# A six-layer fused kernel: causal attention's first sources made inside masked attention, experts' scores reordered by one tile, context loads issued earlier

## The reference, cut to what matters

```python
x = x + cross_attention(norm(x), ctx)          # 16 heads, 257 keys
x = x + state_space(norm(x))
x = x + soft_experts(norm(x))                  # 16 experts x 16 slots
x = x + masked_attention(norm(x), ctx, mask)   # one head, 257 keys
x = x + causal_attention(norm(x))              # 16 heads over 32 rows
x = x + routed_linear(norm(x))                 # one of 8 matrices for a row
```

## Time and profile before

| | us |
|---|---|
| times of the runs shown | 984.61, 985.24, 1930.26 |
| median | 985.24 |
| time of the profiled execution | 986.62 |
| its span | 984.8 |
| TensorE busy | 815.8 (83%) |
| VectorE busy | 726.6 (74%) |
| ScalarE busy | 563.4 (57%) |
| GpSimd busy | 201.6 (20%) |

### The profile page before, as it was taken

One profiled execution on the slowest core, in us unless ns is written; L12 is line 12 of the kernel. 1 busy time (PEld: TensorE's weight loads), 2 busy tenths in 40 slices (PEclk: granted clock), 3 DMA queues, 4 the chain that ended last, 5 costly groups with the idle time before them and its releaser, 6 DMA issues. The chain is left out here.

```text
span 984.8 us, 25493 instructions
## 1 busy us (share of the span) xinstructions
PE 815.8 (83%) x9286; PEld 448.7 (46%) x9286; DVE 726.6 (74%) x2428; ACT 563.4 (57%) x1419; POOL 201.6 (20%) x216
## 2 busy tenths in 40 slices
PE   5899999998867687887764577789698799999887
PEld 2577777776323233333231255456466334343343
DVE  5688888886389999989999588256565376767856
ACT  3798889889666658458415167445243533333345
POOL 1376676666000000000000012000310000000036
PEclk9999999999978789789867799799699899999989
DMA  8111111100000000000000250400183000000001
GB/s 251 34 40 46 37 43 37 38 21 2 1 0 0 1 0 1 1 1 1 0 1 1 82 99 1 173 4 4 44 322 150 1 1 1 1 1 1 1 13 32
DMA packets 23422, 36.67 MB, mean 37 GB/s; under 512 B 5668, under 2 KB 19748, under 8 KB 21156
## 3 DMA queue, kind: packets, MB, share of 16 engines
q1 hardware_dynamic: 23336, 35.53, 11.7%
HBM read 34.48 MB, written 1.05 MB: 36 GB/s over the span
## 5 line engine op out<-in xcount | busy, mean ns | idle before, releaser
L496 ACT ACTIVATE xa_prob<-xa_s,xa_nmax 128x257 f32<-128x257 f32 x256 | 128.1, 503 | 21.0 <-DVE xa_nmax L633 19.3
L780 POOL TENSOR_TENSOR xa_prob<-xa_prob,xa_rinv 128x1028 f32<-128x1028 f32 x64 | 121.6, 1902 | 76.8 <-DVE xa_rinv L640 75.9
L633 DVE CUSTOM_DVE_ANT_0 xa_s<-xa_s_ps,xa_nbias 128x257 f32<-128x257 f32 x256 | 93.1, 420 | 12.4 <-ACT xa_prob L496 6.4
L1764 POOL TENSOR_TENSOR mo_disp_t<-mo_disp_t,mo_rst 128x256 f32<-128x256 f32 x16 | 9.9, 617 | 362.8 <-DVE mo_rst L1734 362.8
L326 PE MATMUL xa_t_ps<-identity,xa_prob 128*128 128x128 f32 x512 | 69.5, 279 | 3.6 <-ACT xa_p_t L505 1.8
L623 DVE COPY xa_kvs<-xa_kv_ps 128x512 f32<-128x512 f32 x64 | 44.1, 689 | 34.4 <-PE xa_kv_ps L300 34.4
L2523 ACT COPY ca_z<-ca_z_ps 128x512 f32<-128x512 f32 x64 | 37.5, 586 | 50.7 <-PE ca_z_ps L2399 50.7
L326 PEld LDWEIGHTS xa_t_ps<-identity,xa_prob 128*128 128x128 f32 x512 | 54.8, 141 | 25.2 <-issue 25.2
L2399 PE MATMUL ca_z_ps<-ca_xn_t,ca_m_t 128*128 128x512 f32 x128 | 64.2, 631 | 0.7 <-ACT ca_xn_t L2516 0.7
L505 ACT COPY xa_p_t<-xa_t_ps 128x1024 f32<-128x1024 f32 x64 | 63.5, 992 | 1.8 <-PE xa_t_ps L326 1.8
L939 PE MATMUL ss_bank<-ss_xs,ss_wx 128*128 128x512 f32 x128 | 60.2, 620 | 5.0 <-DVE ss_eps L1393 3.1
(11 more groups left out here) (369 smaller groups left out, 1898.6 us busy)
## 6 DMA issues: line engine op xcount, KB each, us to landing
xa_ctx_t<-in_ctx_t SPq DMA_DIRECT2D x64, 128.5 KB, 2.1
room<-in_ctx_t SPq DMA_DIRECT2D x8, 1028.0 KB, 6.5
room<-in_ctx_n SPq DMA_DIRECT2D x8, 1024.0 KB, 4.7
ss_wx<-in_ss_wx SPq DMA_DIRECT2D x1, 2048.0 KB, 7.7
xres<-in_x SPq DMA_DIRECT2D x4, 256.0 KB, 5.3
out_x<-xres SPq DMA_DIRECT2D x4, 256.0 KB, 2.3
ma_mask_u<-in_mask SPq DMA_DIRECT2D x4, 128.5 KB
room<-in_ca_wk SPq DMA_DIRECT2D x1, 512.0 KB, 3.5
```

Of the source, the lines that this page charges most:

```text
L496: nc.scalar.activation(prob[:, r, g, :], s_sb[:, b, g, :], ACT.Exp, bias=nmax[:, r, g:g + 1], scale=-1.0, accum_out=rsum[:, r, g:g + 1]).t ...
L633: nc.vector.tensor_tensor_reduce(out=s_sb[:, b, g, :], in0=s_ps[:, g, 0:S], in1=nbias[:, g, :], scale=1.0, scalar=3e38, op0=ALU.add, op1=A ...
L780: nc.gpsimd.tensor_tensor(prob[:, r, :, :], prob[:, r, :, :], bc(rinv[:, r, :].rearrange("p (g o) -> p g o", o=1), (P, G, S)), ALU.mult).t ...
```

## The change

1. Masked attention makes causal attention's inputs for tiles 0 to 3. In slot 5 ScalarE takes Ln and Exp of the variances (`first_scales`), in slot 6 VectorE norms four tiles (`first_rows`), TensorE transposes them (`turn_rows`), ScalarE copies them out, and TensorE makes the 16 sources: two in slot 6, four in slot 7, one ahead of the last `out_weights` and nine behind it. They use masked attention's score banks. `preload_act_table(ACT.Sqrt)` goes.
2. Causal attention starts with `scores(0)`. Its norms use Ln and Exp, only tiles 4 to 15 are normed, and the three remaining `turn_x` stand in slots 0 and 1, as do `normalise(2)`, `normalise(3)` and the bias product.
3. In the experts' scores TensorE, ScalarE and the unit rows run one tile further ahead, GpSimd makes the unit rows in place of ScalarE, `last_squares` stands behind `exps`, and `centred` and `normed` between `maxima` and `scales`. The banks of `l_ps` and of the joins are dealt out anew.
4. The four context loads are issued in this stage, once the last join has read `room`.
5. In the routed layer `own_bias(t)` stands ahead of `experts(t)` for t < 2.

```diff
# masked_attention, TensorE's slot
+                if last:
+                    source(2)
                 key_sums(u, j)
...
+                if not more(u):
+                    if last:
+                        source(3)
+                    else:
+                        turn_rows()
                 turn_c(u)
...
+                if not more(u):
+                    source(4 if last else 0)
                 value_weights(u)
+                if not more(u):
+                    source(5 if last else 1)
...
             steps(pe, slot)
+            source(6)
             pe.wait_ge(res_ready, U - 1)
             out_weights(U - 1, U)
+            for h in range(7, H):
+                source(h)
...
# ScalarE
+            def first_scales():
+                act.wait_ge(eps_set, 1)
+                act.wait_ge(mv_ready, QT // TP)
+                nc.scalar.activation(first.log_var[:, 0:QT], mv[:, 0:QT, 1], ACT.Ln, bias=first.eps[:, :]).then_inc(log_ready, 1)
+                act.wait_ge(log_ready, 1)
+                nc.scalar.activation(rstd[:, 0:QT], first.log_var[:, 0:QT], ACT.Exp, scale=-0.5).then_inc(rstd_ready, 1)
...
+                if isinstance(u, int) and u == U - 3:
+                    first_scales()
...
# VectorE
+            def first_rows():
+                dve.wait_ge(rstd_ready, 1)
+                dve.wait_ge(mv_ready, QT // TP)
+                dve.wait_ge(res_ready, QT // TP)
+                for t in range(QT):
+                    last = nc.vector.tensor_scalar(rows[:, t, :], xres[:, t, :], mv[:, t, 0:1], rstd[:, t:t + 1], ALU.subtract, ALU.mult)
+                last.then_inc(rows_ready, 1)
...
                 turn_p(u)
                 inverse(u, j)
+                if isinstance(u, int) and u == U - 2:
+                    first_rows()
                 if later(u, 1):
                     moments_of(u - 2)
...
# causal_attention, TensorE
                 for half in range(2):
                     for b in range(2 * half, 2 * half + 2):
                         values(t, j, b)
+                    if t == 0 and half == 0:
+                        turn_x(1)
...
                 outputs(t, j)
+                if t < 2:
+                    turn_x(t + 2)
...
-            turn_x(0)
-            for q in range(T // QT):
-                for h in range(HG * q, HG * q + HG):
-                    sources(0, h)
-                if q + 1 < T // QT:
-                    turn_x(q + 1)
             scores(0)
...
# VectorE
-            norm.vector(dve)
-            for q in range(T // QT):
-                normalise(q)
+            dve.wait_ge(own_rstd, 1)
+            nc.vector.scalar_tensor_tensor(nmr[:, QT:T], mv[:, QT:T, 0], -1.0, rstd[:, QT:T], ALU.mult, ALU.mult).then_inc(own_nmr, 1)
+            dve.wait_ge(own_nmr, 1)
+            normalise(1)
+            slot(0, 0)
+            normalise(2)
+            slot(1, 1)
+            normalise(3)
...
-            for t in range(T):
+            for t in range(2, T):
                 slot(t, t % 2)
...
# expert_scores
+        @block.sync
+        def _(sp):
+            sp.wait_ge(join_mm, JOINS)
+            for keys_first in (False, True):
+                for u in range(2):
+                    load_context(sp, d, ctx, u, u, keys_first)
...
             for t in range(T):
-                if t + 2 < T:
-                    turn_x(t + 2, t % 2)
-                turn(t, t % 2)
+                if t + 3 < T:
+                    turn_x(t + 3, 1 - t % 2)
                 if t + 2 < T:
                     logits(t + 2, t % 2)
+                turn(t, t % 2)
...
             for t in range(T):
+                if t + 3 < T:
+                    xut(t + 3, 1 - t % 2)
+                if t + 1 < T:
+                    exps(t + 1, 1 - t % 2)
                 if t == 5:
                     last_squares()
-                if t == 7:
+                if t == 6:
                     last_roots()
-                if t + 2 < T:
-                    xut(t + 2, t % 2)
-                if t + 1 < T:
-                    exps(t + 1, 1 - t % 2)
-                if t + 3 < T:
-                    unit(t + 3, 1 - t % 2)
                 out(t, t % 2)
...
         @block.gpsimd
         def _(pool):
+            def unit(t, j):
+                pool.wait_ge(xut_mm, t - 1)
...
+                nc.gpsimd.tensor_scalar(xu[:, j, :], x1[:, t, :], sums[:, t:t + 1], None, ALU.mult).then_inc(xu_ready, 1)
+
             for t in range(T):
+                if 0 < t and t + 3 < T:
+                    unit(t + 3, 1 - t % 2)
                 pool.wait_ge(rst_ready, t + 1)
```

More of the change, by code:

```diff
@@ L1587, in turn @@
                 last.then_inc(dt_mm, 1)
-            for t in range(2):
-                turn_x(t, t)
-                logits(t, t)
+            turn_x(0, 0)
+            turn_x(1, 1)
+            logits(0, 0)
+            turn_x(2, 0)
+            logits(1, 1)
             for t in range(T):
-                if t + 2 < T:
-                    turn_x(t + 2, t % 2)
-                turn(t, t % 2)
+                if t + 3 < T:
+                    turn_x(t + 3, 1 - t % 2)
                 if t + 2 < T:
                     logits(t + 2, t % 2)
+                turn(t, t % 2)
                 if FIRST <= t < FIRST + JOINS:
@@ L1737, in _ @@
             unit(2, 0)
+            unit(3, 1)
             maxima(0, 0)
@@ L2097, in out_weights, with turn_rows, source @@
                 last.then_inc(out_mm, 1)
+            def turn_rows():
+                pe.wait_ge(rows_ready, 1)
+                pe.wait_ge(qk_ready, U)
+                for i in range(QT):
+                    last = nc.tensor.transpose(f_ps[:, i * P:i * P + P], rows[:, i, :], ident[:, :])
+                last.then_inc(rows_mm, 1)
+            def source(h):
+                if h == 0:
+                    pe.wait_ge(rows_turned, 1)
+                    pe.wait_ge(skeep_ready, TP * U)
+                if h >= 2:
+                    pe.wait_ge(z_ready, h - 1)
+                nc.tensor.matmul(s_ps[:, h % 2, :], m_t[:, h, :], first.xn_t[:, 0:QT, :], start=True, stop=True).then_inc(z_mm, 1)
             def slot(u, j):
+                last = isinstance(u, int) and u == U - 1
                 if more(u):
@@ L2173, in values, with turned_rows, source @@
                 nc.scalar.activation(flat(pv_t[:, :, :]), o_ps[:, 0:TP * P], ACT.Identity, bias=b_v[:, :]).then_inc(pv_ready, 1)
+            def first_scales():
[4 more added lines that the diff above has]
+                nc.scalar.activation(rstd[:, 0:QT], first.log_var[:, 0:QT], ACT.Exp, scale=-0.5).then_inc(rstd_ready, 1)
+            def turned_rows():
+                act.wait_ge(rows_mm, 1)
+                nc.scalar.copy(first.xn_t[:, 0:QT, :].rearrange("p t n -> p (t n)"), f_ps[:, :]).then_inc(rows_turned, 1)
+            def source(h):
+                act.wait_ge(z_mm, h + 1)
+                nc.scalar.copy(first.z[:, h, :], s_ps[:, h % 2, :]).then_inc(z_ready, 1)
             def slot(u, j):
+                last = isinstance(u, int) and u == U - 1
                 last_rows(u)
@@ L2179, in slot @@
                     query_keys(u + 2)
+                if not more(u):
+                    if last:
+                        source(2)
+                        source(3)
+                    else:
+                        turned_rows()
                 turn_c(u)
+                if not more(u):
+                    source(4 if last else 0)
                 values(u)
+                if not more(u):
+                    source(5 if last else 1)
                 if not isinstance(u, int) or u + 3 < U:
@@ L2199, in _ @@
             steps(act, slot, 4)
-            nc.scalar.preload_act_table(ACT.Sqrt)
+            for h in range(6, H):
+                source(h)
         @block.vector
@@ L2280, in _ @@
             norm.vector(dve)
+            nc.vector.memset(first.eps[:, :], EPS).then_inc(eps_set, 1)
             normalise(0)
@@ L2491, in _ @@
         def _(act):
-            norm.scalar(act)
-            nc.scalar.preload_act_table_set("natural_log_exp_and_others")
+            nc.scalar.activation(first.log_var[:, QT:T], mv[:, QT:T, 1], ACT.Ln, bias=first.eps[:, :]).then_inc(own_log, 1)
+            act.wait_ge(own_log, 1)
+            nc.scalar.activation(rstd[:, QT:T], first.log_var[:, QT:T], ACT.Exp, scale=-0.5).then_inc(own_rstd, 1)
             def route_scales():
```

94 lines of the change are left out of this document (50 added, 44 removed).

## The result

The changed kernel takes 962.25 us (960.14 to 965.61, 4 runs), the kernel before 985.11 us in the runs beside it; the ratio is 0.9756, 95% interval 0.9732 to 0.978. The forecast of 974.2 us with a range of 965 to 980 was too slow. One of the four runs of before took 1930.26 us, twice the others; it is left out of the ratio, and without it the median of before is 984.97. The profiled execution took 960.14 us, its span is 958.4.

A forecast was written before the change was run, and what follows sets the result against it. It took VectorE's chain to bound the experts' scores and TensorE causal attention's slots; gains 8.8 + 1.2 + 0.5 + 0.5 = 11.0 us off a median of 985.24 gave 974.2 us, range 965 to 980.

The forecast's parts named there:

- Part 4: Context loads moved out of the expert layers: gain 0.5 us, for TensorE's first pause for instructions only.
- The first reading: Expert layers: the context loads delayed TensorE's instruction fetches and set the series of pauses off.
- the second: Expert layers: TensorE eats 256 instructions faster than they arrive after the stage's start, whatever the loads; taken, 0.5 us gain.
- The rival: Expert layers: the series of pauses goes with the loads, 5 to 8 us more than forecast, about 968; chance 0.28.
- The prediction's own sign of being wrong: Expert layers shorter by over 3 us, listed among the signs that would show the forecast wrong.
- up to 2.6 more: Expert layers: gain beyond 5.7 us of pauses, each 256 instructions taking 4.05 instead of about 5.4 us; chance 0.28.
- Part 3: Experts' scores: reordering covers VectorE's waits for the exponentials' sums; gain 1.2 us, bounds -4.3 and +3.
- I had feared that GpSimd's new instruction would hold VectorE: Experts' scores: GpSimd's `unit` holds VectorE, 3 to 5 us lost, 978; chance 0.10.
- Part 1: Masked attention to tile 0's scores: sources made early, gain 10.9 us, bounds 8 and 12.
- the meeting of the engines: Between ScalarE's last source copy and causal attention's first scores: cost 0.97 us before, expected to stay.
- Part 2: Causal attention's slots 0 and 1: moved transposes and a copy wait lose 2.1 us, bounds 1.5 and 5.
- Part 5: Routed layer's first two tiles: bias product first shortens the 3.70 us ScalarE wait; gain 0.5 us, bounds 0 and 1.

The follow-up runs named there:

- e1_loads: Kernel before, with only the four context loads moved from the expert layers' start to the experts' scores behind the last join; 978.82 us, ratio 0.9936.
- e7_norms_behind: Changed kernel, with `centred` and `normed` put behind `scales` again; experts' scores 55.8 us, for 52.8 in the changed kernel.
- the run at the high level: Changed kernel, with the bias product of the routed layer's first two tiles behind their experts again; routed stage 41.5 us for 41.4.
- e2_sources: Kernel before, with only the first sources inside masked attention and the remaining norms in causal attention's slots; 974.02 us, ratio 0.9893.
- e3_scores: Kernel before, with only the experts' scores reordered and unit rows on GpSimd, context loads left at the expert layers' start; 981.11 us, ratio 0.9959.
- e13_one_mb: Kernel before, with one 1 MB context load at the expert layers' second tile, the other three behind their last tile; expert layers 75.6 us, for 75.5 before.
- e5_loads_mid: Kernel before, with the four context loads issued only from the eighth tile of the expert layers; expert layers 72.9 us, for 75.5 before.
- e11_spread: Kernel before, with the four 1 MB context loads spread over tiles 2, 6, 10 and 14 of the expert layers; 993.05 us, layers 78.2.
- e4_loads_back: Changed kernel, with the four context loads put back to the start of the expert layers; 971.18 us, ratio 0.9854 to the kernel before.

## Why the prediction was wrong

- **Part 4 is the step that failed**: "I take the second and 0.5 us for the first pause". The first reading was right, and moving the loads is worth 7.2 us in the profiles and 6.7 in the median of `e1_loads`. The rival had the mechanism and its price, 5 to 8 us; I gave it 0.28 because five pauses come when the loads are over. That argument was false: a late packet passes its delay on. The DMA rows would have pointed to it ahead of the result, for there was no instruction packet among 3.33 MB, and the next one 2.4 us before the first pause. The prediction's own sign of being wrong, layers shorter by over 3 us, came true. The "up to 2.6 more" of that rival was a slip: five pieces of 5.45 us against 4.05 and the first pause of 0.82 make 7.8, which is 2.1 over the 5.7.
- **Part 3 was mis-sized**: 1.2 us, where the stage gave 4.8, about 4 of them the code's. The wait of 0.30 in four slots was right (`e7_norms_behind`: VectorE's waits rise from 3.2 to 4.4 us). Missing were the collision of the pair with the dispatch product, 4 x 0.33, which stood in my own row as "0.93 for 0.68", and 0.7 for the unit rows. I had feared that GpSimd's new instruction would hold VectorE, and not seen that the pair's new place lets it out of the old hold. `unit` takes 0.60 us, not 0.46, and holds nothing.
- **Part 1 was right**: 10.9 forecast, 11.2 measured, between the same two events. Inside it the last `out_weights` came 3.2 us late, not 4.5 (18.5 us behind slot 5's transposes for 15.3): `first_rows` cost 0.84 instead of 1.5. The nine sources took 8.2 for 7.8, the meeting of the engines 1.02 for 0.97, and the clock rose as I expected with TensorE full. That the total is off by only 0.3 is partly luck: the last `out_weights` was 1.3 us better than forecast, and 0.6 of that went in slots 0 to 4, which the change doesn't touch (54.9 us for 54.4 from the stage's start to slot 5's transposes).
- **Part 2 was nearly right**: slots 0 and 1 lost 2.7 us for 2.1, as a `turn_x` takes 0.66, not 0.5; the wait for the copy was 0.68 for 0.6. Of the other 0.7, 0.3 is the stage's border: the bias product now stands ahead of the product by which I cut.
- **Part 5** gave 0.1 for 0.5, as far as the run at the high level tells; the rest of the stage's 2.4 is the low level of the clock at its start before, or the order at that level, which no run takes apart.

Sum of what the runs put down to the code: 11.2 - 3.4 + 4.1 + 7.2 + 0.1 = 19.2 us, against 11.0 forecast. The medians differ by 22.9. The 3.7 between them I ascribe to the clock (mean 0.933 for 0.915 in the two profiles), in the routed stage above all; that is argued, not shown. By their medians `e1_loads`, `e2_sources` and `e3_scores` gain 6.7, 11.5 and 4.4 us, 22.6 together, so the 3.7 seems to come with parts 1 and 2 (11.5 for 11.2 - 3.4 = 7.8), as far as an interval of some 5 us either way tells.

## What to carry to other kernels

A load that nobody waits for isn't free beside an engine that runs a long program without a loop: look for the instruction packets in the DMA rows, ask when the next one is due, and put the load where the instructions go by slowly (here the scores, where packets stood at 568.1, 584.2 and 608.2 us, and the 4.2 MB of loads from 597.7 to 609.2 us had one of them beside them and cost no pause). Spreading it thinly can be worse than one block at the right place. And where two engines share a slot, read what lies beside an instruction that takes longer than its twins: moving it may pay twice, for the wait it covers and for the neighbour it leaves.

## What the runs showed of the hardware

- One instruction packet 2 to 3 us late cost TensorE six pauses and 7.5 us, over 28 us, with the load over before the first of them (`e13_one_mb`). Why it takes six pieces of 256 instructions to catch up, and none after the longer pause of `e5_loads_mid`, is open; there TensorE ran at the low level behind it.
- A norm of VectorE with two inputs in SBUF was held by GpSimd's product of two inputs (0.93 us for 0.60), and not by GpSimd's `tensor_scalar` of 0.60 us, which overlapped it. The Trainium skill, SBUF — State Buffer, section Who interferes with whom, has a VectorE instruction with two SBUF inputs contend with a GpSimd one that reads SBUF; the product agrees, the `tensor_scalar` doesn't as far as GpSimd's rough spans tell.
- Behind the pause of 2.77 us in `e5_loads_mid` TensorE's clock was 0.54 for 7 us. Behind the pauses of 1.50 us (the kernel before, `e2_sources`) and 1.77 us (`e3_scores`, `e13_one_mb`) it was 0.57 to 0.61 for 4 us, behind that of 2.06 us (`e11_spread`) 0.75, and behind those of 1.41 us and less 1.00. So a part of what the series cost was clock. Busy time behind the second pause of the kernel before (1.50 us) and the third of `e4_loads_back` (1.41 us):

```profile
635.86:639.86 4.00, 4.00 (x75) 2.81 (x78) 0.93 (x4) 1.53 (x6) 0.00 (x0) 0.57 0.01 4
```

```profile
634.78:638.78 4.00, 3.72 (x126) 2.63 (x127) 1.76 (x6) 2.00 (x6) 0.00 (x0) 1.00 0.01 4
```

- In all fifteen profiles masked attention's first 18 us had a mean clock of 0.50 to 0.54, whatever stood ahead of it.
